# Output products of two recurrent layers in half-precision parts

## The reference

```
xn = layernorm(x)
xz = einsum('bhwc,dc->bhwd', xn, w_in)          # 96 -> 384 channels
x_inner, z = split(xz, 2)                       # 192 and 192
step(hprev, gxt):                               # one GRU direction, hidden size 96
    gh = hprev @ whh.T + bhh
    r = sigmoid(gxt[:, :h] + gh[:, :h])
    u = sigmoid(gxt[:, h:2h] + gh[:, h:2h])
    n = tanh(gxt[:, 2h:] + r * gh[:, 2h:])
    return (1 - u) * n + u * hprev
fwd = concat(gru(x_inner), reversed gru(x_inner))        # 192 channels
bwd = flip(concat(gru(flip(x_inner)), reversed gru(flip(x_inner))))
y = silu(fwd + bwd) * silu(z)
x = x + einsum('bld,cd->blc', y, w_out)         # 192 -> 96 channels
```

## Time and profile before

| | us |
|---|---|
| median of 3 runs | 1015.35 (1013.05 to 1015.74) |
| profiled execution | 1011.42 |
| its span | 1009.4 |
| steps of L2, about | 201 to 573.5 |
| output stage of L2 | 576.0 to 591 |
| steps of L3, about | 617.4 to 989.9 |
| output stage of L3, with the last transfer | 992.3 to 1009.4 |

### The profile page before, as it was taken

How to read it: one execution, slowest core, us unless ns; L and a number is a source line. 1 busy time by engine, 2 the same in 40 slices (tenths; PEclk the granted TensorE clock), 3 DMA queues, 4 the chain that set the end, 5 groups by cost and what they waited for, 6 DMA issues and landing times. The chain is left out here.

```text
span 1009.4 us, 54507 instructions
## 1 busy us (share of the span) xinstructions
PE 937.8 (93%) x22226; PEld 831.7 (82%) x22226; DVE 829.4 (82%) x4987; ACT 709.9 (70%) x4622; POOL 47.3 (5%) x24
## 2 busy tenths in 40 slices
PE   4786798699999999999999879999999999999997
PEld 3654687399999999999999747999999999999986
DVE  7754348688888889999999776888889899999993
ACT  4434572577777777888888518777778788888881
POOL 2001241200000000000000030000000000000000
PEclk9687899755555555555555557555555555555555
DMA  5010510000000000000000000000000000000001
GB/s 148 3 18 14 127 32 4 3 5 4 5 4 5 5 4 5 4 5 4 5 4 5 3 6 3 5 5 4 5 4 5 4 5 4 5 4 5 4 5 32
DMA packets 14999, 13.05 MB, mean 13 GB/s; under 512 B 12372, under 2 KB 13909, under 8 KB 14461
## 3 DMA queue, kind: packets, MB, share of 16 engines
q1 hardware_dynamic: 14749, 9.58, 4.0%
HBM read 8.74 MB, written 0.83 MB: 9 GB/s over the span
## 5 line engine op out<-in xcount | busy, mean ns | idle before, releaser
L1288 PE MATMUL L2s_cand_sum<-L_states,L_w_hidden 97*128 97x8 bf16 x2048 | 177.7, 174 | 0.0
L1288 PE MATMUL L3s_cand_sum<-L_states,L_w_hidden 97*128 97x8 bf16 x2048 | 177.3, 174 | 0.0
L1288 PE MATMUL L3s_reset_sum<-L_states,L_w_hidden 97*128 97x8 bf16 x2048 | 141.7, 180 | 2.3 <-DVE L_states L1148 1.6
L1288 PE MATMUL L2s_reset_sum<-L_states,L_w_hidden 97*128 97x8 bf16 x2048 | 141.3, 180 | 2.3 <-DVE L_states L1148 1.6
L1288 PEld LDWEIGHTS L3s_cand_sum<-L_states,L_w_hidden 97*128 97x128 f16 x2048 | 130.5, 104 | 0.0
L1288 PEld LDWEIGHTS L2s_cand_sum<-L_states,L_w_hidden 97*128 97x128 f16 x2048 | 130.4, 104 | 0.0
L1288 PE MATMUL L2s_keep_sum<-L_states,L_w_hidden 97*128 97x8 bf16 x2048 | 130.0, 174 | 0.0
L1288 PE MATMUL L3s_keep_sum<-L_states,L_w_hidden 97*128 97x8 bf16 x2048 | 130.0, 174 | 0.0
L1288 PEld LDWEIGHTS L3s_reset_sum<-L_states,L_w_hidden 97*128 97x128 f16 x2048 | 102.7, 110 | 30.4 <-DVE L_states L1148 4.2
L1288 PEld LDWEIGHTS L2s_reset_sum<-L_states,L_w_hidden 97*128 97x128 f16 x2048 | 102.3, 110 | 30.4 <-DVE L_states L1148 4.2
L1232 ACT ACTIVATE L2s_reset<-L2s_reset_sum 96x16 f32<-96x16 f32 x512 | 93.2, 182 | 45.1 <-PE L2s_reset_sum L1288 45.1
(11 more groups left out here) (252 smaller groups left out, 3123.3 us busy)
## 6 DMA issues: line engine op xcount, KB each, us to landing
L_wih_raw<-in_L_wih SPq DMA_DIRECT2D x2, 1152.0 KB, 11.4
lagged<-in_L_w SPq DMA_DIRECT2D x1, 1296.0 KB, 8.7
L_w_hidden_raw<-in_L_whh SPq DMA_DIRECT2D x2, 576.0 KB
stream<-in_x SPq DMA_DIRECT2D x2, 384.0 KB, 3.7
out<-stream SPq DMA_DIRECT2D x4, 192.0 KB, 2.1
l_idft<-in_idft SPq DMA_DIRECT2D x1, 400.0 KB
rpe_lw<-in_rpe_lw SPq DMA_DIRECT2D x1, 384.0 KB
lagged<-coefs SPq DMA_DIRECT2D x16, 24.0 KB, 2.0
```

The costliest lines, as they stand in the source:

```text
L1288: return e.matmul(dst, weights.hidden[0:rows, wp, GATES * (2 * g + j) + gate, :], rhs, start=False, stop=False, skip_group_check=True)
```

## The change

The two fp32 products of each token group in `gru_output` become six products of half-precision operands, three for each half of the channels: high part of the tokens times high part of w_out, high times low, low times high. The parts of w_out are made in `gru_input`, the high one by ScalarE between the last `weight_low` and the gates, the low one by VectorE behind its other work. The parts of the tokens are made in `gru_steps`: `high_part` on ScalarE in slots 10 to 13, `low_part` on VectorE in slots 12 to 15, and both for the last 8 steps behind the last step. They are written interleaved into the memory of y, whose words are no longer needed by then: high part in one half of a word, low part in the other, so that the tokens of one part lie two elements apart. The core of the diff:

```diff
@@ gru_layer
         w_out = sbo("w_out", [C, CHUNKS, C])
+        w_out_parts = sbo("w_out_parts", [C, 2, CHUNKS, C], F16)
+        s_parts = y[:].bitcast(F16).rearrange("p m b (t k) -> p m b t k", k=2)
@@ gru_input, vector
+                e.wait_ge(w_parted, 2 * W_BANKS + 2)
+                e.tensor_tensor(w_out_parts[:, 1], w_out[:], w_out_parts[:, 0], ALU.subtract)
@@ gru_input, scalar
                 for b in range(W_BANKS):
                     weight_low(b)
+                e.wait_ge(w_loaded, 16)
+                e.activation(w_out_parts[:, 0], w_out[:], ACT.Copy).then_inc(w_parted, 1)
@@ gru_steps, vector
+                def low_part(q, i):
+                    m, at = part(q, i)
+                    e.wait_ge(hi_parted, count(q, i))
+                    e.tensor_tensor(s_parts[:, m, :, at:at + STEPS, 1], of_tokens(s_tok, q, i), s_parts[:, m, :, at:at + STEPS, 0],
+                                    ALU.subtract).then_inc(lo_parted, 1)
+
                 def beside(g, q):
                     n, before = 2 * (q % STEPS) + g, q - q % STEPS - STEPS
-                    if before >= SEQ // 2 and n < 12:
-                        (add_directions, apply_y, apply_gate)[n // 4](before, n % 4)
+                    if before >= SEQ // 2:
+                        (add_directions, apply_y, apply_gate, low_part)[n // 4](before, n % 4)
...
-                for work in (add_directions, apply_y, apply_gate):
+                for work in (add_directions, apply_y, apply_gate, low_part):
                     for i in range(4):
                         work(SEQ - STEPS, i)
-                e.wait_ge(gated, count(SEQ - STEPS, 3))
+                e.wait_ge(lo_parted, count(SEQ - STEPS, 3))
@@ gru_steps, scalar
+                def high_part(q, i):
+                    m, at = part(q, i)
+                    e.wait_ge(gated, count(q, i))
+                    e.activation(s_parts[:, m, :, at:at + STEPS, 0], of_tokens(s_tok, q, i), ACT.Copy).then_inc(hi_parted, 1)
@@ between
                     if q >= SEQ // 2 + STEPS and 4 <= 2 * s + g < 8:
                         sigmoid_of_y(q - s - STEPS, 2 * s + g - 4)
+                    if q >= SEQ // 2 + STEPS and 10 <= 2 * s + g < 14:
+                        high_part(q - s - STEPS, 2 * s + g - 10)
...
                 for i in range(4):
                     sigmoid_of_y(SEQ - STEPS, i)
+                for i in range(4):
+                    high_part(SEQ - STEPS, i)
@@ gru_output, tensor
-                e.wait_ge(w_loaded, 16)
-
                 for k in range(NB):
                     h = k // 2
                     for t in range(4):
                         for m in range(CHUNKS):
-                            last = e.matmul(banks[k][:, t * C:(t + 1) * C], s_tok[:, m, 4 * (k % 2) + t, half_of(h)],
-                                            w_out[:, m, :], start=(m == 0), stop=(m == CHUNKS - 1))
+                            tokens = s_parts[:, m, 4 * (k % 2) + t, half_of(h)]
+                            for n, (sp, wp) in enumerate(((0, 0), (0, 1), (1, 0))):
+                                last = e.matmul(banks[k][:, t * C:(t + 1) * C], tokens[:, :, sp], w_out_parts[:, wp, m, :],
+                                                start=(m == 0 and n == 0), stop=(m == CHUNKS - 1 and n == 2))
                     last.then_inc(projected, 1)
```

More of the change, by code:

```diff
@@ L920, in gru_layer, with gru_input @@
             forward = sb("forward", [C + 1, 2, BATCH, SEQ], F16)
[L921 to L926, removed]
+            gru_input(nc, d, layer, stream, ident, weights, forward, states, gate, w_out, w_out_parts, w_loaded, stats)
+            gru_steps(nc, layer, weights, forward, states, gate, y, s_tok, s_parts)
+        gru_output(nc, layer, stream, s_parts, w_out_parts, stats, out_dram, stored)
+def gru_input(nc, d, layer, stream, ident, weights, forward, states, gate, w_out, w_out_parts, w_loaded, stats):
     with ExitStack() as ctx:
@@ L1046, in _, with gru_steps @@
                     last.then_inc(projected, 1)
-def gru_steps(nc, layer, weights, forward, states, gate, y, s_tok):
+def gru_steps(nc, layer, weights, forward, states, gate, y, s_tok, s_parts):
     with ExitStack() as ctx:
@@ L1092, in gru_steps @@
         y_ready, factors, gated = sem("y_ready"), sem("factors"), sem("gated")
+        hi_parted, lo_parted = sem("hi_parted"), sem("lo_parted")
         def part(q, i):
@@ L1325, in _, with gru_output @@
                         add(KEEP, 0, 1, 1).then_inc(keep_summed[g], 1)
-def gru_output(nc, layer, stream, s_tok, w_out, w_loaded, stats, out_dram, stored):
+def gru_output(nc, layer, stream, s_parts, w_out_parts, stats, out_dram, stored):
     with ExitStack() as ctx:
```

## The result

| | before | after |
|---|---|---|
| median, us | 1015.55 (4 runs, 1013.05 to 1016.11) | 1000.71 (4 runs, 998.24 to 1003.22) |
| ratio | 1 | 0.9867, 95% interval 0.9834 to 0.9901 |
| profiled execution, its span | 1011.42, 1009.4 | 1003.22, 1001.2 |

What follows compares the result with a forecast made beforehand. TensorE was taken to bound the output stages, the step's chain and TensorE the recurrences. -7.4 + 1.1 + 0.3 + 0.55 = -5.4 us off the median 1015.35 gave 1010 us, range 1007 to 1012.5 (8 in 10: 1006 to 1022).

Steps and rivals of the forecast that it cites:

- Part 1: Output products: 64 fp32 become 192 half-precision a layer, stage 13.94 to 10.25 us, saving 3.7 a layer, 7.4 in all.
- three passes stream more columns: Output stage at half clock: 192 x 0.080 = 15.4 us of columns against 64 x 0.160 = 10.2 for fp32.
- the prices: Output stage, per 96-column half-precision product: 0.080 us at half clock, 0.0435 at full clock, loads hidden.
- The clock: Output stage: gapless columns raise TensorE's clock from 1.2 to 2.4 GHz 3.7 us into the stage.
- Rival A: Output stages: clock stays at 1.2 GHz, 15.7 us a stage, +5.5 with costs, 1020.8 us; chance 0.12.
- rival B: Output stages: strided weight loads are slow, columns wait, clock does not rise, 20.9 us a stage, 1031 us; chance 0.07.
- So 1.5 a bank of 3.4, under the 2.1 us of a faster bank: L2's output stage: VectorE's addition and statistics per bank stay shorter than TensorE's bank of 48 products.
- Part 2: Tail between last step and output: last copy and subtraction add 0.54 us a layer, 1.1 for two.
- Part 3: Recurrence steps: 120 copies and 120 subtractions ride in existing slots, costing 0.3 us; bounds nothing and 55 us.
- Rival D: Recurrence steps: strided half-precision writes outlast their slots, at 0.40 us a copy +10, 1026 us; chance 0.05.
- Part 4: Input stage: ScalarE's 0.36 us copy of w_out adds 0.27 a layer on the path, 0.55 in all.
- The range: Total time: own range 1007 to 1012.5 us; for 8 in 10, 1006 to 1022.

Runs made afterwards that it cites:

- kernel of 192 products: Kernel after the change with each of its 96 products a layer made twice, also called the doubled kernel; 1009.57 us, ratio 0.9935.
- one-pass kernel: Kernel after the change with the product of the high parts alone, 32 products a layer; 997.3 us, ratio 0.9822.
- kernel of 127 weights: Kernel after the change with five of each group's six products on 127 of the 128 tokens; 1006.95 us, ratio 0.9934.
- the parts alone: Kernel after the change with the output products put back to fp32, half-precision parts made but not used; 1015.5 us, ratio 1.0006.
- the two streams of 24: Kernel before with 24 half-precision products of 512 columns between each layer's last step and the fp32 output; 1011.96 us, ratio 0.9969.
- 12 products ahead of fp32: Kernel before with 12 half-precision products of 512 columns between each layer's last step and the fp32 output; 1018.88 us, ratio 1.0042.

## Why the prediction was wrong, point by point

**Part 1, the count: this is the step that failed.** "64 fp32 products become 192 in half precision, per layer." They are 32, and become 96. With 96 at the prediction's own prices: 3.7 us at the half clock are 46 products, the other 50 take 50 x 0.0435 = 2.2, and 0.2 for the drain, 6.1 us a stage. That saves 13.94 - 6.1 = 7.8 a layer, 15.7 in two, less 1.95 of costs: 13.7, or 1015.35 - 13.7 = 1001.6 us where 1000.71 was measured. That it comes so near is partly luck: the output stages gave 0.8 us less than that and the tails took 0.4 more, and the input stages and steps, where 0.85 of cost was forecast, were 1.0 shorter. The kernel of 192 products shows the same from the other side. The trace of before had the evidence: line 1014 has three banks and two halves, six products, and the earlier trace rows hold three groups of x4, twelve records; line 1044 has eight banks of half-precision products with three combinations, and the earlier trace rows hold x24, one record each. A count from the trace was never set against the loops of the code.

**Part 1, "three passes stream more columns": the wrong way round.** The price by column, fp32 at twice half precision, was the price of one of the two records. An fp32 product of 512 columns takes two records of 0.853 us at the half clock, 1.71, against 0.427 for half precision: four to one. Per layer the columns' time at the half clock is 32 x 2 x 0.160 = 10.2 us before and 96 x 0.080 = 7.7 after, a quarter less and not half more. The Trainium skill (FP8 and Floating Point Precision, section TensorE Precision Notes) says four passes for true fp32; by that rule three passes save a quarter. The prediction wrote "This trace disagrees", and that was its error: the trace agrees, with two records of twice the length each.

**Part 1, the prices: right.** At the half clock 0.080 a product was said; the one-pass kernel has (2.72 - 0.28)/31 = 0.0787. At the full clock 0.0435 was said; of the doubled kernel's 10.41 us, 4.5 lie before the rise (a mean clock of 0.55 in 586 to 587), which is 57 products, and the other 135 take 10.41 - 4.5 - 0.21 = 5.7, or 0.0422. The loads take 143 ns and 97 ns at the two levels, and overlap: they hold nothing up.

**The clock: right in kind, late by 0.6 and 1.1 us.** Taken: 3.7 us into the stage; measured 4.3 and 4.8. Each microsecond more at the lower level costs 1 - 0.0435/0.080 = 0.46, so 0.3 and 0.5 us, less the somewhat better pace: 6.26 and 6.48 against the 6.1 above. (By its own prices a rise one us earlier gives 9.8, not 9.7.) Rival A, no rise, did not happen in any stage of three passes with 128 weights a load; rival B's condition, columns waiting for slow loads, is what the kernel of 127 weights has, and it behaved as B said: no rise.

**"So 1.5 a bank of 3.4, under the 2.1 us of a faster bank": wrong with the count.** A bank is 24 products, 1.05 us at the full clock, and VectorE needs 0.55 + 0.74 = 1.29, where 1.5 was read from a window that held more than one bank's work. VectorE is now the bound of L2's output behind the rise, worth 1.88 - 1.67 = 0.2 us between the last product and the next stage.

**Part 2, the tail: right in L3, short in L2.** Said 0.54 a layer. L3 has 0.5 more by the table, L2 1.0, of which 0.46 is VectorE idle between the last new_state and the first addition, in the trace above; before it was 0.11. The kernels with the parts alone, the doubled products and 127 weights all have L2's tail at 3.7, so it belongs to the code of the change; its cause was not looked for.

**Part 3, the slots: right.** Zeroings are (404.2 - 218.9)/16 = 11.58 us apart ahead of chunk 17 and (556.3 - 405.0)/13 = 11.64 behind it, where before had 11.60 and 11.63: 0.06 us a chunk for the twenty-four operations, against 0.03 for the sixteen before, and the steps as a whole did not lengthen (373.4 and 373.3 against 373.6 and 373.3). The new copy takes 0.263 us and the subtraction 0.223, under the 0.27 at which the prediction put the first loss. Rival D is out.

**Part 4, w_out's copy: right and then hidden.** It takes 0.37 us, said 0.36, and runs straight into the table load at 609.39. The input stage of L3 is nonetheless 24.4 us against 24.7. Its length goes with the clock: the clock rose 13.3 us into the stage, against 14.3 before; in the kernel with the parts alone it rose 12.7 us in and the stage has 24.1 us, in the one-pass kernel 15.7 and 25.5.

**The range.** It took its lower end from an earlier rise and the scatter, and no chance was kept for a miscount. A check of 64 against the loops would have cost a line and moved the forecast by 8 us.

## What to carry to other kernels

Before a count of records enters a sum, divide it by the count in the loops: here an fp32 product is two records on TensorE and on its load queue (an fp32 transpose is one), so a change of type changes the number of records to a product. Where a page's rule and a trace seem to disagree by a factor of two, look for that factor in what one row stands for before saying which is wrong. And take a stage that was bound by TensorE through again with the new time of a bank: VectorE, at 1.29 us, became the bound as soon as a bank fell below it.

## What the hardware showed that was not expected

- A load of 127 half-precision weights takes 0.224 us and one of 128 takes 0.143, both at 1.2 GHz; through the slower pace and the clock that did not rise, this made the two output stages 3.5 us longer each (11.6 against 8.1, 13.1 against 9.6).
- The time from a stream's start to the rise of the clock scatters: 3.7 to 4.8 us over the eight output stages of three passes behind loads of 128, 3.6 and 6.0 in the two streams of 24, 7.0 in L1's fp32 products above, and in one kernel, that of 12 products ahead of fp32, 5.28 us of gapless 512-column products passed in both layers without a rise. The Trainium skill (TensorE: Matmul & The Clock Gate, section The HAM clock gate) lets the moment of the rise vary by half a microsecond either way; the spread here is wider, and the traces decide.
- The fp32 products of the output stage, 96 columns behind 128 weights, did not raise the clock in 13.9 us in any kernel here, but kept it when a stream ahead had raised it: the same 32 products in 7.36 us. In the kernel after, L1's fp32 products of 192 columns behind 128 weights did raise it, at 129.4 us.
- The stretch ahead of L2 has two lengths, 175 and 181 us. Between before and after, 3.3 us of it lie where the clock is up at 87 or at 95 us, 2.1 where it is up at 118 or at 129, and the rest ahead of both. That scatter is larger than the effect of the smaller edits, and the reason to compare profiles from a stage's start.
